# A token mixer written out by batch: norm and shortcut each one pass on ACT, biases of a PSUM bank laid by one product

## What is computed

```python
x = x + _L0_attn_a_ref(_layernorm(x, axis=-1), Wq, bq, Wk, bk, Wv, bv, Wo, bo)
...
def _L1_attn_b_ref(x, Wu, bu, Wv, bv, Wo, bo, zero, pos):
    n, b, e = x.shape
    shortcut = x
    xn = _simple_rmsnorm(x)
    u = jax.nn.silu(jnp.einsum('nbe,de->nbd', xn, Wu) + bu)
    v = jax.nn.silu(jnp.einsum('nbe,de->nbd', xn, Wv) + bv)
    vh = v.transpose(1, 0, 2).reshape(b, n, H, HD).transpose(0, 2, 1, 3)
    oh = _toeplitz_causal_fft(vh, zero, pos)
    o = oh.transpose(0, 2, 1, 3).reshape(b, n, D1).transpose(1, 0, 2)
    o = u * o
    return jnp.einsum('nbd,ed->nbe', o, Wo) + bo + shortcut
...
x = x + _L1_attn_b_ref(_layernorm(x, axis=-1), ...)
```

## Time and profile before

| | |
|---|---|
| median of 3 runs | 1863.72 us (1859.49 to 1864.86) |
| the profiled execution | 1868.03 us |
| its span, first to last instruction | 1866.3 us |
| mean granted TensorE clock | 0.841 of full speed |
| busy: PE, DVE, ACT, POOL | 1338.2, 1087.7, 749.7, 827.1 us |

### The profile page before, as it was taken

How to read it: one execution, slowest core, us unless ns; L and a number is a source line. 1 busy time by engine, 2 the same in 40 slices (tenths; PEclk the granted TensorE clock), 3 DMA queues, 4 the chain that set the end, 5 groups by cost and what they waited for, 6 DMA issues and landing times. The chain is left out here.

```text
span 1866.3 us, 36265 instructions
## 1 busy us (share of the span) xinstructions
PE 1338.2 (72%) x11228; PEld 869.7 (47%) x11229; DVE 1087.7 (58%) x3234; ACT 749.7 (40%) x1222; POOL 827.1 (44%) x1189
## 2 busy tenths in 40 slices
PE   5873249963988888832499638888899976957485
PEld 3652139961233333321499613333355545634364
DVE  2564435545887777343355466675766625759764
ACT  1221113311466666611133116676655543634153
POOL 2105745533233333357455347676644403446242
PEclk9795569985799999955699858998999997978688
DMA  3004122245333222041222400000000000000001
GB/s 102 0 1 126 45 61 68 68 118 128 66 83 80 64 64 64 3 128 43 64 66 68 117 19 1 1 2 1 1 2 2 1 2 1 1 1 1 1 1 45
DMA packets 87713, 79.80 MB, mean 43 GB/s; under 512 B 11792, under 2 KB 77584, under 8 KB 87281
## 3 DMA queue, kind: packets, MB, share of 16 engines
q1 hardware_dynamic: 76898, 57.16, 12.0%
q0 software_dynamic: 8704, 17.97, 2.9%
q10 hardware_dynamic: 1980, 3.00, 0.8%
HBM read 46.07 MB, written 32.01 MB: 42 GB/s over the span
## 5 line engine op out<-in xcount | busy, mean ns | idle before, releaser
L1146 ACT ACTIVATE grp_pt<-ps 128x1024 f32<-128x1024 f32 (+2 forms) x320 | 244.6, 799 | 213.6 <-PE ps L1223 135.2
L2035 DVE TENSOR_REDUCE soft_mx<-ps 128x2 f32<-128x1024 f32 (+3 forms) x256 | 201.8, 820 | 58.8 <-PE ps L1873 57.5
L680 POOL DMA_INDIRECT products<-moe_product,moe_rows_in x144 | 153.2, 1064 | 148.2 <-DVE moe_product L852 143.4
L1759 ACT ACTIVATE soft_pt<-ps 128x768 f32<-128x768 f32 (+1 forms) x192 | 166.3, 884 | 83.4 <-PE ps L1904 81.8
L1680 POOL TENSOR_SCALAR_AFFINE_SELECT soft_pt<-soft_pt 128x256 f32<-128x256 f32 (+1 forms) x192 | 92.7, 483 | 210.8 <-ACT soft_pt L1759 210.2
L707 ACT ACTIVATE moe_hid<-ps 128x512 f32<-128x512 f32 x144 | 86.0, 597 | 246.3 <-PE ps L744 246.3
L744 PE MATMUL ps<-moe_rT,moe_W_now 128*128 128x128 f32 x1152 | 157.1, 281 | 1.7 <-issue 1.5
L1243 PE MATMUL ps<-grp_pt,grp_vpad 128*32 128x160 f32 (+4 forms) x2048 | 146.1, 394 | 15.8 <-POOL grp_pt L1088 15.7
L753 PE MATMUL ps<-moe_W,moe_hid 128*128 x1152 | 154.8, 278 | 0.0
L658 POOL DMA_INDIRECT sorted_rows<-moe_row,moe_target x128 | 124.8, 975 | 50.2 <-issue 34.6
L744 PEld LDWEIGHTS ps<-moe_rT,moe_W_now 128*128 128x128 f32 x1152 | 143.3, 196 | 4.7 <-issue 4.6
(11 more groups left out here) (333 smaller groups left out, 2808.5 us busy)
## 6 DMA issues: line engine op xcount, KB each, us to landing
moe_rows_in<-sorted_rows SPq DMA_DIRECT2D x144, 65.0 KB, 1.8
moe_back<-products SPq DMA_DIRECT2D x16, 512.0 KB, 7.2
soft_kst<-soft_scratch_k SPq DMA_DIRECT2D x32, 192.0 KB
moe_W<-in_W SPq DMA_DIRECT2D x2, 2048.0 KB, 8.4
moe_W<-in_W SPq DMA_DIRECT2D x16, 256.0 KB, 7.0
soft_scratch_q<-soft_parts SPq DMA_DIRECT2D x16, 192.0 KB, 2.7
soft_qst<-soft_scratch_q SPq DMA_DIRECT2D x32, 96.0 KB
soft_scratch_k<-soft_parts SPq DMA_DIRECT2D x14, 192.0 KB, 2.7
```

What stands on the lines that cost most here:

```text
L680: pool.indirect_dma_start(k.products, bass.IndirectOffsetOnAxis(rows_in[:, u, DEST_COL:DEST_COL + 1].bitcast(U32), 0), product[:, u, :], N ...
L1146: act.activation(at.pair(pt[:, s % 2, :], pair, seg)[:, :, 0:w], ring[(chunks_before(m) + c) % 2][:, :, 0:w], ACT.Exp, scale=scale).then_i ...
L1759: act.activation(LATENT.pair(pt[:, s % 2, :], pair, seg)[:, :, 0:w], ring[second_turn(n, c) % RING3][:, :, 0:w], ACT.Exp, scale=scale).the ...
L2035: ins = dve.tensor_reduce(mx[:, tile, half, :, r], ring[first_turn(n, d) % RING3][:, :, at:at + keys], AX.X, ALU.max)
```

## The change

Linear attention: the bias products are laid first, over a whole bank at once by a broadcast operand, and the products are added to them. The one for the output stands ahead of the wait for `aT`. The last product of each group is then the data's, no longer the bias's.

The mixer no longer uses `Norm` and `Feed`; all is written out for the eight batches:

- DVE: `stats` run two batches ahead; no normalisation; taps go from the oldest v to the newest, so v of batch n comes last; gates wait for their own u.
- POOL: `power(n)` has twelve steps instead of seven and makes four columns for each tile: scale and shift for the projection's entry, scale and shift for the shortcut (x times (rstd + 1) minus mean times rstd). These have two halves, n % 2, and so `power(n)` waits for `shortcut` of n - 2. The shortcut is not POOL's any more.
- ACT: `entries(n)` makes the entry tiles from x by one instruction each, with scale and bias columns; `shortcuts(n)` does the same in place on x. SiLUs come in the order v, v, u, u.
- PE: `turn` runs ahead; the order is turn(n + 2), project(n + 1), output(n). The output has one bank, so `output(n)` waits for the addition of n - 1. Its bias is laid by one product of 512 columns; then come the eight products, half by half.

The core of the diff (the allocation of buffers and counters, the SiLU and copy functions and the removed lines of the mixer are left out):

```diff
@@ -364,9 +364,10 @@
                 pe.wait_ge(phi.sem, phi.at(n - 1))
                 pe.matmul(ps_q, k.WqT, feed.xT[:, p, :], start=True, stop=True).then_inc(q_ready.sem, 1)
                 pe.wait_ge(v_ready.sem, v_ready.at(n - 1))
-                for j in range(T):
-                    pe.matmul(kv_view[:, j, :], feed.xT[:, p, j * P:(j + 1) * P], k.WkvT, start=True, stop=False)
-                    ins = pe.matmul(kv_view[:, j, :], k.onesb, k.bkv_rows, start=False, stop=True)
+                for b in range(2):
+                    pe.matmul(ps_kv[:, b, :], k.onesb, k.bkv_rows.unsqueeze(1).to_broadcast([P, 2, 2 * P]), start=True, stop=True)
+                for j in range(T):
+                    ins = pe.matmul(kv_view[:, j, :], feed.xT[:, p, j * P:(j + 1) * P], k.WkvT, start=False, stop=True, skip_group_check=True)
                 ins.then_inc(kv_ready.sem, 1)
 
             def sums(n, p):
@@ -389,11 +390,10 @@
                 for j in range(T):
                     ins = pe.transpose(ps_sum[:, j * P:(j + 1) * P], quot[:, j, :], k.ident)
                 ins.then_inc(q_turned.sem, 1)
+                pe.matmul(ps_out, k.onesb, k.bo_rows.unsqueeze(1).to_broadcast([P, T, P]), start=True, stop=True)
                 pe.wait_ge(aT_ready.sem, aT_ready.at(n))
                 for j in range(T):
-                    o = ps_out[:, j * P:(j + 1) * P]
-                    pe.matmul(o, aT[:, p, j * P:(j + 1) * P], k.WoT, start=True, stop=False)
-                    ins = pe.matmul(o, k.onesb, k.bo_rows, start=False, stop=True)
+                    ins = pe.matmul(ps_out[:, j * P:(j + 1) * P], aT[:, p, j * P:(j + 1) * P], k.WoT, start=False, stop=True, skip_group_check=True)
                 ins.then_inc(out_ready.sem, 1)
 
             def body(n, p, n_back, p_back):
@@ -2327,129 +2327,221 @@
...
+            def power(n):
+                p = n % 2
+                mean, var = mv[:, p, :, 0], mv[:, p, :, 1]
+                pool.wait_ge(stats_done.sem, stats_done.at(n))
+                need(pool, powered, powered.at(n - 1))
+                need(pool, shortcut, shortcut.at(n - 2))
+                pool.tensor_scalar(tmp[:, :], var, 1e-5, None, ALU.add).then_inc(powered.sem, 1)
+                pool.wait_ge(powered.sem, powered.at(n, 1))
+                pool.tensor_tensor(rstd[:, :], tmp[:, :], half[:, 0, :], ALU.pow).then_inc(powered.sem, 1)
+                pool.wait_ge(powered.sem, powered.at(n, 2))
+                pool.tensor_tensor(tmp[:, :], var, rstd[:, :], ALU.mult).then_inc(powered.sem, 1)
+                pool.wait_ge(powered.sem, powered.at(n, 3))
+                pool.tensor_tensor(tmp[:, :], tmp[:, :], rstd[:, :], ALU.mult).then_inc(powered.sem, 1)
+                pool.wait_ge(powered.sem, powered.at(n, 4))
+                pool.tensor_tensor(tmp[:, :], tmp[:, :], half[:, 1, :], ALU.pow).then_inc(powered.sem, 1)
+                pool.wait_ge(powered.sem, powered.at(n, 5))
+                pool.tensor_scalar(tmp[:, :], tmp[:, :], 1e-8, None, ALU.add).then_inc(powered.sem, 1)
+                pool.wait_ge(powered.sem, powered.at(n, 6))
+                pool.tensor_tensor(factor[:, :], tmp[:, :], half[:, 2, :], ALU.pow).then_inc(powered.sem, 1)
+                pool.wait_ge(powered.sem, powered.at(n, 7))
+                pool.tensor_tensor(in_scale[:, p, :], rstd[:, :], factor[:, :], ALU.mult).then_inc(powered.sem, 1)
+                pool.wait_ge(powered.sem, powered.at(n, 8))
+                pool.tensor_scalar(tmp[:, :], mean, -1.0, None, ALU.mult).then_inc(powered.sem, 1)
+                pool.wait_ge(powered.sem, powered.at(n, 9))
+                pool.tensor_tensor(in_shift[:, p, :], tmp[:, :], in_scale[:, p, :], ALU.mult).then_inc(powered.sem, 1)
+                pool.tensor_tensor(x_shift[:, p, :], tmp[:, :], rstd[:, :], ALU.mult).then_inc(powered.sem, 1)
+                pool.tensor_scalar(x_scale[:, p, :], rstd[:, :], 1.0, None, ALU.add).then_inc(powered.sem, 1)
+
...
+            def entries(n):
+                p = n % 2
+                act.wait_ge(powered.sem, powered.at(n))
+                need(act, x_turned, x_turned.at(n - 2))
+                for j in range(T):
+                    ins = act.activation(entry[:, p, j, :], k.x[:, n * T + j, :], ACT.Identity, bias=in_shift[:, p, j:j + 1], scale=in_scale[:, p, j:j + 1])
+                ins.then_inc(normed.sem, 1)
+
+            def shortcuts(n):
+                p = n % 2
+                act.wait_ge(normed.sem, normed.at(n))
+                for j in range(T):
+                    x = k.x[:, n * T + j, :]
+                    ins = act.activation(x, x, ACT.Identity, bias=x_shift[:, p, j:j + 1], scale=x_scale[:, p, j:j + 1])
+                ins.then_inc(shortcut.sem, 1)
+
...
+            entries(0)
+            copy_xT(0)
+            entries(1)
             for n in range(B):
                 if n + 1 < B:
...
+                    copy_xT(n + 1)
+                silus(n)
+                shortcuts(n)
+                if n + 2 < B:
+                    entries(n + 2)
...
+            def turn(n):
+                pe.wait_ge(normed.sem, normed.at(n))
+                need(pe, xT_ready, xT_ready.at(n - 1))
+                for j in range(T):
+                    ins = pe.transpose(ps_x[:, j * P:(j + 1) * P], entry[:, n % 2, j, :], k.ident)
+                ins.then_inc(x_turned.sem, 1)
+
+            def project(n):
+                pe.wait_ge(xT_ready.sem, xT_ready.at(n))
+                for i, c in enumerate(OUTPUTS):
+                    need(pe, silu_ready, silu_ready.at(n - 1, i + 1))
+                    pe.matmul(ps_uv[c], k.WuvT[:, c * P:(c + 1) * P], xT[:, n % 2, :], start=True, stop=True).then_inc(uv_ready.sem, 1)
+
+            def output(n):
+                need(pe, x_added, x_added.at(n - 1))
+                pe.matmul(ps_out, k.onesb, k.bto_rows.unsqueeze(1).to_broadcast([P, T, P]), start=True, stop=True)
+                for c in range(FEAT):
+                    pe.wait_ge(gated_ready.sem, gated_ready.at(n, c + 1))
+                    for j in range(T):
+                        ins = pe.matmul(ps_out[:, j * P:(j + 1) * P], gated[:, n % 2, c, j * P:(j + 1) * P], k.WtoT[:, c * P:(c + 1) * P],
+                                        start=False, stop=True, skip_group_check=True)
+
+            turn(0)
+            turn(1)
+            project(0)
+            for n in range(B):
+                if n + 2 < B:
+                    turn(n + 2)
+                if n + 1 < B:
+                    project(n + 1)
+                output(n)
...
+            def mix(n):
+                need(dve, gated_ready, gated_ready.at(n - 1))
+                for i, lag in enumerate(range(n, -1, -1)):
+                    for c in range(FEAT):
+                        at = c * B + lag
+                        v, scale = vT[:, c, n - lag, :], k.coef[:, at:at + 1]
+                        dve.wait_ge(silu_ready.sem, v_ready(n - lag, c))
+                        if i > 0:
+                            dve.wait_ge(taps[c].sem, counts[c])
+                            dve.scalar_tensor_tensor(mixed[:, c, :], v, scale, mixed[:, c, :], ALU.mult, ALU.add).then_inc(taps[c].sem, 1)
+                            counts[c] += 1
+                        else:
+                            dve.tensor_scalar(mixed[:, c, :], v, scale, None, ALU.mult).then_inc(taps[c].sem, 1)
+                            counts[c] += 1
+
+            def gate(n):
+                need(dve, out_ready, out_ready.at(n - 2))
+                for c in range(FEAT):
+                    dve.wait_ge(silu_ready.sem, silu_ready.at(n, OUTPUTS.index(c) + 1))
+                    dve.wait_ge(taps[c].sem, counts[c])
+                    dve.tensor_tensor(gated[:, n % 2, c, :], mixed[:, c, :], uT[:, n % 2, c, :], ALU.mult).then_inc(gated_ready.sem, 1)
+
+            def add(n):
+                x = x_of(n).rearrange("p a b -> p (a b)")
+                dve.tensor_tensor(x, ps_out, x, ALU.add).then_inc(x_added.sem, 1)
+
+            stats(0)
+            stats(1)
+            for n in range(B):
+                if n + 2 < B:
+                    stats(n + 2)
+                mix(n)
+                gate(n)
+                if n > 0:
+                    add(n - 1)
+            add(B - 1)
```

More of the change, by code:

```diff
@@ L2360, in token_mixer @@
-        block = st.block()
-        def batches(front, back):
-            front(0, 0)
+        exps = st.counter("exponents", 3)
+        stats_done = st.counter("stats_done", 2)
+        powered = st.counter("power_steps", 12)
+        normed = st.counter("normed")
+        shortcut = st.counter("shortcut")
+        x_turned = st.counter("x_turned")
+        xT_ready = st.counter("xT_ready")
+        uv_ready = st.counter("uv_ready", 4)
+        silu_ready = st.counter("silu_ready", 4)
+        taps = [st.counter(f"taps{c}") for c in range(FEAT)]
@@ L2450, in _ @@
-            norm.stats(dve, 0, 0)
-            batches(lambda n, p: feed.vector(dve, n, p), back)
```

(3 more changed lines are left out.)

138 lines of the change are left out of this document (53 added, 85 removed).

## The result

The changed kernel takes **1898.28 us** (median of 4 runs, 1895.69 to 1901.3), the kernel before 1864.26 us (4 runs, 1859.49 to 1864.86). The ratio is 1.0189, with a 95% interval of 1.0166 to 1.0212: 34 us slower, where 42 were forecast. The profiled execution took 1897.72 us, its span is 1895.4 us, the mean granted clock 0.841.

A forecast was written before the change was run, and what follows sets the result against it. The mixer was taken as DVE's: a start bound by the norm, then taps. Mixer +47.7 us and linear attention -5.3 gave +42.4, so 1906 us from the 1863.7 median; range 1887 to 1920.

The forecast's parts named there:

- The ring: Mixer: project, SiLUs, shortcuts, power, entries, turn, next project follow one another almost without overlap; six rounds of 18.3 us.
- The mixer's sum: Mixer: start, six rounds and end together make the stage 47.7 us longer.
- the start: Mixer's beginning: POOL does two power chains back to back, so the first projection starts at 1658.5 instead of 1652.59.
- S(0): S(n) is when ACT ends batch n's last SiLU; S(0) was forecast at 1665.8, S(6) at 1775.6.
- the tail: Mixer's end: DVE's last work and the one-bank output(7) follow S(6), ending 20.0 us later at 1795.6.
- POOL beside taps: Mixer's power chain: 5.9 us alone, 8.7 beside DVE's taps; about half lies beside taps, so 7.3 taken.
- Linear attention: the term of the sum: Linear attention: output bias laid during PE's wait saves 0.92 or 0.5 us a batch, 5.3 us taken.
- k and v bias "nothing": Linear attention's k and v products: same bias columns and bound by columns, so no gain.
- A: Rival, mixer: PE stays at 2.4 GHz, rounds take 16.0 us, total 1890; chance 0.12.
- B: Rival, mixer: POOL is shut out while taps run, power averages 9.2 us, total 1917; chance 0.12.
- C: Rival, mixer: the ring does not bind, DVE stays the bound, total falls to 1839; chance 0.03.
- D: Rival, mixer: power overlaps the SiLUs, rounds take 11 us, total within a few us of before; chance 0.03.

The follow-up runs named there:

- four sets: The changed kernel with four sets of scale and shift instead of two, so power(n) waits for the shortcut of n - 4: 1857.76 us.
- shortcut first: The changed kernel with shortcuts(n) moved ahead of silus(n) on ACT: 1870.65 us.
- turn late: The changed kernel with turn(n + 2) behind project(n + 1) and output(n) on PE: 1886.35 us.
- early start: The changed kernel with four scale and shift sets, PE's projections ahead of turns, and batch 0's SiLUs ahead of batch 1's copy on ACT: 1852.26 us.
- linear attention alone: The kernel before with only the change's two linear-attention edits, the mixer left as before: 1861.91 us.
- 9 filling products: The changed kernel with 9 more 512-column products on PE behind output(n) for n = 0 to 4, into an unread bank: 1899.48 us.

## Why the prediction was right, and where its sizes were off

**The ring: right.** Its edges are the ones named (waits above), its rounds are nearly even, and each edit that takes a part out of the ring shortened the stage by tens of us (four sets 46.7, shortcut first 29.7, turn late 20.0). A round was forecast at 18.3 us and took 17.6:

| step of the round | forecast | measured, mean |
|---|---|---|
| shortcuts | 1.64 | 1.64 |
| power | 7.3 | 7.1 (5.8 to 8.1) |
| entries | 1.64 | 1.65 |
| turn | 1.12 | 0.91, start to start |
| project to the last SiLU | 6.3 | 6.2 |
| hand-overs | 0.3 | 0.15 |

**The mixer's sum: 7.0 us too high.** 4.2 are the six rounds at 0.7 us: a turn priced by its end, where the projection begins 0.2 us before it, 0.2 of power, 0.15 of hand-overs (the shortcuts begin 0.1 us before the recorded end of the last SiLU) and 0.1 of projection. 1.4 are the start (S(0) 20.6 us behind POOL's first step, forecast 21.95), mostly its projection, 6.5 us to the last SiLU where the old 7.3 was taken over. 1.3 are the tail (18.7 us from S(6), forecast 20.0; the output of batch 5 ran at 2.4 GHz, 1.95 us, and not between the clocks).

**POOL beside taps: the size was right, and in part by luck.** The whole chain was 1.4 times its length at most (8.1 against 5.8 us), the mean came out at 7.1, and in this stage no step was more than 0.4 us longer than its like alone. But the forecast read the trace of before too mildly: besides the step of 1.66 us it has one of 2.60 at 1680.07 where its like takes 1.01, and the seven steps around it took 6.83 us, not 6.21. Such steps, 1.6 us and more, came in six other profiles too (1.81 with four sets and in "early start", 3.23 in "shortcut first"), each with DVE's two-input gates beside it. In the changed kernel no gate met the chain: POOL starts when ACT's shortcuts are over, and in all six rounds the gates were over 1 us before (the first time at 1652.92, POOL at 1653.91). The forecast had said that POOL starts behind the gates, and did not say that this was what kept long steps away.

The Trainium skill's page "SBUF — State Buffer" (section "Summary: rules for kernel authors") says that a VectorE instruction with two SBUF inputs and a GpSimd instruction that reads SBUF exclude each other, the second waiting until the first is over. These runs do not decide it: 0.4 us more beside a train of taps is less than one tap of 0.67, and the step of 3.23 us is longer than four.

**Linear attention: the term of the sum was mis-sized, -5.3 forecast, -8.8 measured**, and its reason with it. The products themselves gave 0.2 us a batch at 2.4 GHz (1.38 to 1.16), not 0.5: the eight passes did not come at half of their slow 1.7 us. Slow, they took 1.9 us (70.14 to 72.01, where the turn begins), so the saving there was 0.75 and not 0.92. The rest is the clock, which the forecast had left at "may cost or give a few us". At 2.4 GHz a batch takes 10.16 us against 10.3 before, so eight such batches would save 1 us; the gain is that more of them have it. Which edits go with a higher clock is seen (the clocks above), but not why less work in a batch raises it: with or without the change PE's busy share in 60 to 80 us is high (17.4 us of 20 before, 15.7 after, 15.1 with linear attention alone). That stays open.

**k and v bias "nothing": right for the products, wrong for the stage.** At 2.4 GHz the four products and their bias take 2.17 us before (103.82 to 105.99) and 2.16 after (85.00 to 87.16). The stage with this edit alone is still 3 to 5 us shorter (104.9 against 108.0 and 110.3), with the clock at 0.91 instead of 0.74 to 0.79 in 80 to 100 us; in the total nothing can be told.

**The rivals.** A, a fast clock throughout: no, the clock was 0.59 in turn and projection; the run with 9 filling products shows what it would have brought, 9.2 us of the 14 + 2 worked out, in five of the six rounds. B, POOL shut out: not in the changed kernel, 7.1 us and not 9.2; in "shortcut first" one chain of 11.8 us was of its kind. C and D: no, ACT waits for POOL in every round.

**The sign and the range** (1887 to 1920) held; the two errors, 7.0 us in the mixer and 3.5 in linear attention, both lay on the high side, and the untouched stages, counted as 0, were 2.4 us shorter in the one profile.

## What to carry to other kernels

Before columns or buffers are made by batch, go once round the engines' in-order queues: where the reader of batch n's set stands last in ACT's queue and the writer of batch n + 2's set feeds the next thing in it, two halves turn a pipeline into a ring, and the price is the sum of its steps, however idle each engine looks. Here two more halves of 128x4 columns were worth 47 us. When one ring is cut, look for the next (what does the moved instruction wait for, and who stands behind it?) before moving a second thing.

## What the runs showed of the hardware that was not expected

- A PE that was busy for 6.89 of 6.9 us from 1661.4, behind 9.94 us of idleness, was granted half of its clock for the first 4.6 us and 0.59 over the whole. With the gap filled (1.47 us left) the same work ran at 1.00.
- In linear attention a slightly lighter batch went with another clock: 0.74 in 60 to 80 us of the span before, 0.84 in the changed kernel, 1.00 in the kernel with linear attention alone.
- A GpSimd step on 128x4 elements that takes 0.22 us alone took 3.23 beside VectorE's last taps and gates; beside taps without gates such a step took at most 0.72.
- A float32 product of 512 columns is two passes of 0.43 us each at 2.4 GHz (36 passes in 15.62 us, and 8 in 3.60).
